# Attention's first blocks stored by two queues and turned sooner, its maxima and queries summed in PSUM, the projections' tiles normalised by ScalarE

## The chip, the cores and the metric

One core of a Trainium2 chip runs the whole program in one launch. Its engines are TensorE (PE), VectorE (DVE), ScalarE (ACT), GpSimd (POOL) and SyncE (SP), which only issues transfers; each works through its own instructions in order and waits on semaphores for the others. The metric is the device time of one execution in microseconds.

## The reference

Four layers, each between a layer norm before and one after, added to the residual. The change touches only the first, attention over 2 sequences of 512 tokens and 32 heads of 16:

```python
x = x + _layernorm(_L0_attn_ref(_layernorm(x), wq, wk, wv, wo))
# _L0_attn_ref, b=2, s=512, H=32, HD=16
q = rotary((x @ wq).reshape(b, s, H, HD)); k = rotary((x @ wk).reshape(b, s, H, HD))
v = (x @ wv).reshape(b, s, H, HD)
scores = jnp.einsum('bqhd,bkhd->bhqk', q, k) * scale
scores = jnp.where(causal[None, None], scores, jnp.finfo(scores.dtype).min)
out = jnp.einsum('bhqk,bkhd->bqhd', jax.nn.softmax(scores, axis=-1), v).reshape(b, s, d)
return out @ wo
```

After it come a feed-forward layer with low-rank terms, a recurrent mixer of four layers, and a feed-forward layer with 4-bit weights.

## The kernel before

Products are made of three fp32r products of a high and a low part (hi·hi, hi·lo, lo·hi), so each operand is split: ScalarE copies it to fp32r, and VectorE or GpSimd subtracts that copy from the source.

**Projections.** Tokens are 8 tiles of 128. For tile t VectorE makes mean and variance (`stats`), GpSimd the inverse deviation (`inv_std`), VectorE the normalised tile `xn` (`norm_x`), TensorE turns it (L1264), ScalarE and VectorE split it into `xt_hi` and `xt_lo`, and TensorE makes q, k and v with 12 products each (L1271), one tile's 36 products two tiles behind the turning. VectorE rotates q and k in two parts (`rope`, L930 and L935) and GpSimd adds them into `qk`, three tiles behind. The weights wq, wk, wv are split in between: the high parts by ScalarE, the low ones by VectorE (L950), one in each of its steps 2, 3 and 4.

**Blocks and stacks.** A block g holds four pairs of heads for all 512 tokens of one sequence, 8 blocks in all, 32 pairs. TensorE turns q and k of a block (`turn_block`, L1277), ScalarE copies the high part (`turned_hi`) and VectorE the low one (`turned_lo`). Twelve transfers store them to `turned` in HBM, each part twice or three times in other rows, and GpSimd's queue loads the result as two tiles of 1 MB with hi and lo stacked over 64 rows (`load_stacks`), so that one product of 64 rows gives a score of all parts. Block 0 is turned within the projections, before the last two tiles (banks 6 and 7); SP stores it, and GpSimd loads it after its last addition to `qk`. It goes to `q_first` and `k_first`, the others to `xt_hi` and `xt_lo`.

**The loop.** `PERIODS` is one list for all engines: each takes from it, in its order, the steps that concern it. A period m works on four pairs: ONE (scores of a tile of queries, with a mask, L1322 and L1326, of which VectorE takes the maxima, L970) for the next two pairs; TWO (transposed scores less the maxima, L1367) for the two pairs now, of which ScalarE takes the exponential (L797) and GpSimd zeroes the corner above the diagonal (L701); PV (probabilities times v, L1378), FLIP (turning the result back, with VectorE's division), TURN (turning half a block, into bank 6) and STACK (loading a block). ONE, TWO and FLIP share a ring of three pairs of banks, and each waits for the reader of the step three before. PLACE brings a pair's maxima under its queries: TensorE multiplies the rows of maxima, `max_row`, with the identity into bank 6 (L1359), and VectorE adds the stack of queries and writes `q_less_max` (L983, out as `w_hi`), which TWO reads. The loop begins with m = −1, where there is only ONE for pairs 0 and 1 and the turning of block 1.

## Time and profile before

| what | us |
|---|---|
| median of 3 runs (868.88, 877.41, 869.16) | 869.16 |
| profiled execution | 873.33 |
| its span in the trace | 871.6 |
| TensorE busy in the span | 763.8 (88%) |
| VectorE | 580.2 (67%) |
| GpSimd | 436.9 (50%) |
| ScalarE | 321.6 (37%) |
| attention, from the start to the last product of its loop | about 310 |
| short steps: VectorE's two on the maxima | 0.21 and 0.17 |
| ScalarE's copy of v, of the identity | 0.60, 0.30 |
| VectorE's remainder of half a block (128x512) | 0.69 |

The span is the time between the first and the last instruction in the trace. Busy times overlap between engines, so shares say who is loaded, and the chain of waits says who is waited for. A row of the timeline gives start, length, engine, line, operation, out<-in with shapes, and in brackets how long the engine had been idle and who ended it. A matmul's recorded length is longer than the step to the next one, since they overlap in the array; so for a series the step between starts counts. "fp32r" products of 512 columns come one after another at 0.23 us.

### The profile page before, as it was taken

To read this page: it belongs to the slowest core of one execution; us is meant where nothing else is said; L and a number is where in the kernel's file an instruction comes from. 1 tells how busy PE (TensorE), PEld (TensorE's weight loads), DVE (VectorE), ACT (ScalarE), POOL (GpSimd) and SP (SyncE) were. 2 spreads that over 40 slices of the span, in tenths; PEclk is the share of its full clock that TensorE was granted. 3 is DMA by queue.
4 is the path that set the end of the run, shared out by engine and by line. 5 is a ranking of instruction groups with operands and counts; after the bars stand their busy time and mean duration, and the time that the engine had idled before them with its cause. 6 is when DMAs were issued, how large, how long until landed. Compare 5 with 4: busy or idle time off the path is not lost.

```text
span 871.6 us, 12853 instructions
## 1 busy us (share of the span) xinstructions
PE 763.8 (88%) x4451; PEld 552.9 (63%) x4451; DVE 580.2 (67%) x1251; ACT 321.6 (37%) x535; POOL 436.9 (50%) x587
## 2 busy tenths in 40 slices
PE   3799688999999887868998898989988999999995
PEld 2578454555555355646886676766766776778883
DVE  5444275888888449996447887889787777580015
ACT  3011044555555544423322432432353342524420
POOL 3233222354333226446645765765686586566632
PEclk9899867999999879979999999999999999999998
DMA  8001463545552040345484332431644131234301
GB/s 304 0 1 34 136 197 121 185 148 155 165 170 97 2 162 1 115 142 184 172 288 161 124 124 91 133 121 63 190 132 121 34 89 48 61 97 145 88 1 48
DMA packets 56944, 101.38 MB, mean 116 GB/s; under 512 B 13616, under 2 KB 17200, under 8 KB 54704
## 3 DMA queue, kind: packets, MB, share of 16 engines
q1 hardware_dynamic: 54576, 83.78, 30.6%
q0 software_dynamic: 2304, 16.78, 5.3%
q8 instruction: 36, 0.59, 0.3%
q14 instruction: 28, 0.23, 0.1%
HBM read 74.58 MB, written 27.00 MB: 117 GB/s over the span
## 4 chain that ended last, share of the span: by engine, by line
PE 54%; DVE 30%; issue 5%; POOL 4%; ACT 4%; DMA 3%; SPq 0%; DVEq 0%; ACTq 0%; POOLq 0%
PE psum L1456 18%; PE psum L1476 11%; PE psum L1271 7%; DVE negmax L970 5%; PE psum L1378 3%; PE psum L1367 3%; DVE bnst L1038 2%; ACT probs L797 2%; DVE w_hi L983 2%; DVE stage_w L1130 2%; PE psum L1507 2%; DVE hn L1210 1%; PE psum L1322 1%; DVE x L1051 1%; DMA xt_lo<-turned 1%
## 5 line engine op out<-in xcount | busy, mean ns | idle before, releaser
L1456 PE MATMUL psum<-xt_hi,wgu_hi 128*128 128x512 f32 (+1 forms) x352 | 142.7, 405 | 0.0
L1456 PE MATMUL psum<-xt_hi,wgu_lo 128*128 128x512 f32 (+1 forms) x352 | 141.8, 403 | 0.0
L1456 PE MATMUL psum<-xt_lo,wgu_hi 128*128 128x512 f32 (+1 forms) x352 | 141.3, 401 | 0.0
L725 POOL TENSOR_TENSOR wgu_lo<-raw,wgu_hi 128x512 fp32r<-128x512 f32 (+1 forms) x88 | 116.9, 1335 | 32.3 <-ACT wgu_hi L857 32.1
L970 DVE TENSOR_REDUCE negmax<-psum 128x2 f32<-128x1024 f32 (+3 forms) x128 | 104.0, 820 | 33.6 <-PE psum L1326 31.6
L701 POOL TENSOR_SCALAR_AFFINE_SELECT probs<-probs 128x256 f32<-128x256 f32 x128 | 52.1, 407 | 140.1 <-ACT probs L797 140.0
L797 ACT ACTIVATE probs<-psum 128x1024 f32<-128x1024 f32 (+3 forms) x128 | 89.0, 704 | 86.2 <-PE psum L1367 84.6
L1109 DVE TENSOR_TENSOR hf<-sg,psum 128x512 f32<-128x512 f32 (+1 forms) x44 | 30.0, 683 | 81.7 <-PE psum L1456 55.2
L725 POOL TENSOR_TENSOR wd_lo<-raw,wd_hi 128x512 fp32r<-128x512 f32 (+1 forms) x44 | 58.2, 1333 | 40.3 <-ACT wd_hi L864 40.1
L730 POOL TENSOR_TENSOR h_lo<-hf,h_hi 128x512 fp32r<-128x512 f32 (+1 forms) x44 | 59.1, 1344 | 37.1 <-ACT h_hi L878 37.1
L1476 PE MATMUL psum<-wd_hi,h_hi 128*128 128x512 f32 (+1 forms) x176 | 73.4, 417 | 4.2 <-POOL h_lo L730 3.7
L1456 PEld LDWEIGHTS psum<-xt_hi,wgu_lo 128*128 128x128 f32 (+1 forms) x352 | 66.4, 189 | 16.6
L1456 PEld LDWEIGHTS psum<-xt_hi,wgu_hi 128*128 128x128 f32 (+1 forms) x352 | 66.3, 188 | 15.4 <-POOL wgu_lo L725 0.2
L1456 PEld LDWEIGHTS psum<-xt_lo,wgu_hi 128*128 128x128 f32 (+1 forms) x352 | 66.3, 188 | 15.1
L857 ACT ACTIVATE wgu_hi<-raw 128x512 fp32r<-128x512 f32 (+1 forms) x88 | 53.2, 616 | 46.4 <-PE psum L1456 24.2
L1476 PE MATMUL psum<-wd_hi,h_lo 128*128 128x512 f32 (+1 forms) x176 | 70.2, 399 | 0.0
L1476 PE MATMUL psum<-wd_lo,h_hi 128*128 128x512 f32 (+1 forms) x176 | 70.0, 398 | 0.0
L1378 PE MATMUL psum<-probs,v 128*32 128x128 f32 (+3 forms) x512 | 51.6, 477 | 4.3 <-POOL probs L701 3.6
L1367 PE MATMUL psum<-w_hi,xt_lo 64*128 64x512 f32 (+2 forms) x224 | 46.3, 412 | 5.4 <-DVE w_hi L983 3.7
L670 POOL TENSOR_TENSOR qk<-rot_c,rot_s 128x512 f32<-128x512 f32 x16 | 21.1, 1316 | 57.1 <-DVE rot_s L935 57.1
L878 ACT ACTIVATE h_hi<-hf 128x512 fp32r<-128x512 f32 (+1 forms) x44 | 27.7, 630 | 57.6 <-DVE hf L1109 56.7
L710 POOL TENSOR_SCALAR ve<-mv 128x1 f32<-128x1 f32 x56 | 16.2, 290 | 63.2 <-DVE mv L1039 36.7
(202 smaller groups left out, 1581.7 us busy)
## 6 DMA issues: line engine op xcount, KB each, us to landing
raw<-full SPq DMA_DIRECT2D x60, 256.0 KB, 2.7
raw<-in_gu_t SPq DMA_DIRECT2D x40, 256.0 KB, 3.8
stage_w<-in_w SPq DMA_DIRECT2D x30, 256.0 KB, 3.2
full<-stage_w SPq DMA_DIRECT2D x30, 256.0 KB, 2.0
turned<-w_hi SPq DMA_DIRECT2D x56, 128.0 KB, 3.4
xt_hi<-turned POOLq DMA_DIRECT2D x7, 1024.0 KB, 5.1
xt_lo<-turned POOLq DMA_DIRECT2D x7, 1024.0 KB, 7.7
turned<-w_lo SPq DMA_DIRECT2D x28, 128.0 KB, 2.4
```

The costliest lines, as they stand in the source:

```text
L701: nc.gpsimd.affine_select(out=diagonal, in_=diagonal, pattern=[[0, 2], [1, P]], compare_op=ALU.is_ge, fill=0.0, base=0, channel_multiplier ...
L725: nc.gpsimd.tensor_tensor(lo, src, hi.bitcast(F32), ALU.subtract).then_inc(sem("w_lo"), 1)
L730: nc.gpsimd.tensor_tensor(h_lo[0:n, r % RING, :], hf[0:n, r % 2, :], h_hi[0:n, r % RING, :].bitcast(F32), ALU.subtract).then_inc(sem("h_lo ...
L797: nc.scalar.activation(probs_of(e)[:, :, 0:(TB - i) * P], pair_of_banks(e)[:, :, 0:(TB - i) * P], ACT.Exp).then_inc(sem("exp"), 1)
L857: nc.scalar.activation(wgu_hi[:, (2 * r + c) % 4, :, 0:n], src.rearrange("p (k h) -> p k h", k=KD)[:, :, 0:n], ACT.Copy).then_inc(sem("w_h ...
L970: nc.vector.tensor_reduce(negmax[:, g, i, :], pair_of_banks(e)[:, :, 0:(i + 1) * P], AX_X, ALU.max, negate=True).then_inc(sem("row_max"), 1)
L1109: nc.vector.tensor_tensor(hf[0:n, r % 2, :], sg[0:n, r % 2, :], bank[(2 * r + 1) % 3][0:n, :], ALU.mult).then_inc(sem("full"), 1)
L1271: ins = nc.tensor.matmul(dst, lhs(i, k), rhs(j, k), start=start and n == 0, stop=stop and n == len(todo) - 1)
L1367: ins = nc.tensor.matmul(pair_of_banks(e)[:, h, 0:(TB - i) * P], k_stack(g)[rows, i * P:(i + 1) * P], q_less_max(g)[rows, i * P:S], start= ...
L1378: ins = nc.tensor.matmul(bank[7][32 * four:32 * four + 32, i * P:S], v[:, TB * b + i, col:col + 32], probs_of((TWO, pair, i))[:, h, 0:(TB ...
L1456: ins = nc.tensor.matmul(bank[q % 3][0:n, :], (wgu_hi, wgu_lo)[hi_w][:, q % 4, k, 0:n], XT[hi_x][:, k, ch * 512:ch * 512 + 512], start=ite ...
L1476: ins = nc.tensor.matmul(bank[3 + j % 2][:, :], (h_hi, h_lo)[lo_h][0:n, r % RING, j * P:(j + 1) * P], (wd_hi, wd_lo)[lo_w][0:n, r % RING, ...
```

## The change

1. ScalarE makes `xn` instead of VectorE, as x·rstd + (−mean·rstd); GpSimd computes the bias in one more step (`ve[:, 7]`). ScalarE's order is: tile t+1 normalised, then tile t copied.
2. The stores of blocks 0 and 1 are split: SP issues the six of q (j = 0), ScalarE's queue the six of k (j = 1). Later blocks stay with SP.
3. GpSimd loads block 0 before its last two additions to `qk`, instead of after them.
4. Both halves of block 1 are turned at once at the loop's start, into banks 6 and 7, and its load is taken up at the start of period 0.
5. PLACE: TensorE first multiplies the stack of queries with the identity into bank 6 and adds the maxima to it there; ScalarE copies the sum. VectorE's addition is gone.

```diff
-            ahead = 1 if m < 0 else m // 2 + 2 if m % 2 == 0 else 0
+            ahead = m // 2 + 2 if m >= 0 and m % 2 == 0 else 0
             stack = m // 2 + 1 if m % 2 == 0 else 0
-            todo = [(STACK, stack * (m > 0), 0), (TWO, now_a, 0), (ONE, next_a, 3), (PLACE, now_b, 0),
+            todo = [(TURN, int(m < 0), 0), (TURN, int(m < 0), 1), (STACK, stack, 0), (TWO, now_a, 0), (ONE, next_a, 3), (PLACE, now_b, 0),
                     (TWO, now_a, 1), (ONE, next_a, 2), (PV, m - 1, 3), (TWO, now_b, 0), (TURN, ahead, 0), (ONE, next_a, 1),
-                    (STACK, stack * (m == 0), 0), (TWO, now_b, 1), (ONE, next_a, 0), (PV, m, 0), (TURN, ahead, 1),
+                    (TWO, now_b, 1), (ONE, next_a, 0), (PV, m, 0), (TURN, ahead, 1),
...
+        def turn_bank(g, i):
+            return bank[6 + i if g == 1 else 6]
...
+        def store_turned(queue, G, j, part):
+            block, ready = ((turned_hi(G), "block_hi"), (turned_lo(G), "block_split"))[part]
+            queue.wait_ge(sem(ready), 2 * G + j if G else 1)
+            for h in range(2):
+                for copy in range(3):
+                    if part == (copy == 2 - j):
+                        row = 64 * h + HD * copy
+                        queue.dma_start(turned[G % 2, j, row:row + HD].rearrange("r p n -> (r p) n"),
+                                        block[64 * h:64 * h + 64, j, :].bitcast(F32)).then_inc(sem(f"turned_out{G % 2}"), 16)
...
+                for part in range(2):
+                    for j in range(2 if G > 1 else 1):
+                        store_turned(sp, G, j, part)
...
-                nc.gpsimd.tensor_tensor(rstd[:, n, t:t + 1], ve[:, n, t:t + 1], neghalf[:, 0:1], ALU.pow).then_inc(sem(done), 1)
...
+                link(nc.gpsimd.tensor_tensor(rstd[:, n, t:t + 1], ve[:, n, t:t + 1], neghalf[:, 0:1], ALU.pow))
+                nc.gpsimd.tensor_scalar(ve[:, 7, t:t + 1], mv[:, n, t, 0:1], rstd[:, n, t:t + 1], -1.0, ALU.mult, ALU.mult).then_inc(sem(done), 1)
...
+                if t == NT + ROPE_LAG - 1:
+                    pool.wait_ge(sem("stack_rows_in"), 8 * 16)
+                    load_stacks(0)
...
-            pool.wait_ge(sem("stack_rows_in"), 8 * 16)
-            load_stacks(0)
...
+            def norm_x(t):
+                act.wait_ge(sem("x_rstd0"), t + 1)
+                if t >= 2:
+                    act.wait_ge(sem("xt_psum0"), t - 1)
+                nc.scalar.activation(xn[:, t % 2, :], x[:, t, :], ACT.Identity, bias=ve[:, 7, t:t + 1], scale=rstd[:, 0, t:t + 1]).then_inc(sem("xn0"), 1)
+
+            norm_x(0)
             for t in range(NT + 2):
+                if t + 1 < NT:
+                    norm_x(t + 1)
                 if t < NT:
                     xt_tile(0, t)
...
                     nc.scalar.activation(turned_hi(0), psum[:, 6:8, :], ACT.Copy).then_inc(sem("block_hi"), 1)
+                    store_turned(act, 0, 1, 0)
+                    store_turned(act, 0, 1, 1)
...
+                    if g == 1 and i == 1:
+                        store_turned(act, 1, 1, 0)
+                        store_turned(act, 1, 1, 1)
...
+                elif what == PLACE:
+                    act.wait_ge(sem("placed"), g + 1)
+                    nc.scalar.activation(q_less_max(g), bank[6][:, :], ACT.Copy).then_inc(sem("q_less_max"), 1)
...
-                elif what == PLACE:
-                    dve.wait_ge(sem("placed"), g + 1)
-                    nc.vector.tensor_tensor(q_less_max(g), bank[6][:, :], q_stack(g).bitcast(F32), ALU.add).then_inc(sem("q_less_max"), 1)
...
+                    nc.tensor.matmul(bank[6][:, :], ident_r[:, :], q_stack(g), start=True, stop=False)
                     for t in range(TB):
-                        ins = nc.tensor.matmul(bank[6][:, t * P:(t + 1) * P], max_row[:, t, :], ident_r[:, :], start=True, stop=True)
+                        ins = nc.tensor.matmul(bank[6][:, t * P:(t + 1) * P], max_row[:, t, :], ident_r[:, :], start=False, stop=t == TB - 1)
```

Where the instructions stand, first on TensorE at the end of the projections, before (L1271 projections, L1322 and L1326 scores of pair 0 with mask, L1277 the turning of block 1's first half):

```order
L1271 MATMUL psum<-w_hi,xt_lo 128x512
L1322 MATMUL psum<-k_first,q_first 128x512 x2
L1326 MATMUL psum<-causal,ident 128x128 x2
L1326 MATMUL psum<-causal,ident 128x64 x2
L1322 MATMUL psum<-k_first,q_first 128x384 x2
L1326 MATMUL psum<-causal,ident 128x128 x2
L1326 MATMUL psum<-causal,ident 128x64 x2
L1277 MATMUL psum<-ident,qk 128x128 x4
```

and now (L1284, L1335 and L1339, L1290 in the same order):

```order
L1284 MATMUL psum<-w_hi,xt_lo 128x512
L1290 MATMUL psum<-ident,qk 128x128 x8
L1335 MATMUL psum<-k_first,q_first 128x512 x2
L1339 MATMUL psum<-causal,ident 128x128 x2
L1339 MATMUL psum<-causal,ident 128x64 x2
L1335 MATMUL psum<-k_first,q_first 128x384 x2
```

The eight transposes of block 1 have moved ahead of all scores. On GpSimd at the same place, before (L670 additions to qk, L682 loads of blocks 0 and 1, L701 corner of the probabilities):

```order
L670 TENSOR_TENSOR qk<-rot_c,rot_s 128x4x4x32 x8
L682 DMA q_first<-turned 128x2048
L682 DMA k_first<-turned 128x2048
L701 AFFINE_SELECT probs<-probs 128x2x128 x3
L682 DMA xt_hi<-turned 128x2048
L682 DMA xt_lo<-turned 128x2048
```

and now (L694, L676, L710):

```order
L694 TENSOR_TENSOR qk<-rot_c,rot_s 128x4x4x32 x6
L676 DMA q_first<-turned 128x2048
L676 DMA k_first<-turned 128x2048
L694 TENSOR_TENSOR qk<-rot_c,rot_s 128x4x4x32 x2
L676 DMA xt_hi<-turned 128x2048
L676 DMA xt_lo<-turned 128x2048
L710 AFFINE_SELECT probs<-probs 128x2x128 x16
```

The load of block 0 has moved ahead of the last two additions, and that of block 1 ahead of the first three corners. On TensorE within a period of the loop, around the placing of a pair's maxima, before (L1359 the placing, L1367 transposed scores):

```order
L1322 MATMUL psum<-xt_lo,xt_hi 128x384 x2
L1326 MATMUL psum<-causal,ident 128x128 x2
L1326 MATMUL psum<-causal,ident 128x64 x2
L1359 MATMUL psum<-ident_r,max_row 128x128 x4
L1367 MATMUL psum<-w_hi,xt_lo 128x128 x2
L1322 MATMUL psum<-xt_lo,xt_hi 128x256 x2
```

and now (L1371 the queries, L1373 the maxima, L1381 transposed scores):

```order
L1335 MATMUL psum<-xt_lo,xt_hi 128x384 x2
L1339 MATMUL psum<-causal,ident 128x128 x2
L1339 MATMUL psum<-causal,ident 128x64 x2
L1371 MATMUL psum<-xt_hi,ident_r 128x512
L1373 MATMUL psum<-ident_r,max_row 128x128 x4
L1381 MATMUL psum<-w_hi,xt_lo 128x128 x2
L1335 MATMUL psum<-xt_lo,xt_hi 128x256 x2
```

One product of 512 columns has been added ahead of each placing; there are 32 of them.

## Rows read from the trace of the kernel before

**Rows 1.** Timeline of the projections: start, length, engine, line, operation, [idle <-releaser]

```profile
15.70 1.12 PE L1264 MATMUL psum<-ident,xn 128*128 128x128 f32 x4 [3.09 <-DVE xn L914]
30.05 0.80 PE L1271 MATMUL psum<-w_hi,xt_hi 128*128 128x512 f32 x1 [5.88 <-DVE w_lo L950]
44.11 0.66 PE L1264 MATMUL psum<-ident,xn 128*128 128x128 f32 x4 [0.31 <-DVE xn L914]
11.24 0.61 POOL L656 TENSOR_TENSOR rstd<-ve,neghalf 128x1 f32<-128x1 f32 x1
11.96 2.27 DVE L950 TENSOR_TENSOR w_lo<-w_raw,w_hi 128x2048 fp32r<-128x2048 f32 x1
26.41 0.79 DVE L914 TENSOR_SCALAR xn<-x,mv,rstd 128x512 f32<-128x512 f32 x1
```

**Rows 2.** Timeline, end of the projections: stores and load of block 0

```profile
82.56 7.52 SPq L570 DMA_DIRECT2D turned<-y  x12
97.64 0.40 PE L1271 MATMUL psum<-w_lo,xt_hi 128*128 128x512 f32 x1
97.87 0.40 PE L1271 MATMUL psum<-w_hi,xt_lo 128*128 128x512 f32 x1
98.17 0.79 POOL L682 DMA_DIRECT2D q_first<-turned  x1
106.09 0.80 PE L1322 MATMUL psum<-k_first,q_first 64*128 64x512 f32 x2 [7.82 <-DMA k_first<-turned]
```

**Rows 3.** Timeline, maxima of pairs 0 and 1, first transposed scores

```profile
107.18 2.09 DVE L970 TENSOR_REDUCE negmax<-psum 128x2 f32<-128x1024 f32 x2 [9.78 <-PE psum L1326]
110.12 1.01 DVE L970 TENSOR_REDUCE negmax<-psum 128x2 f32<-128x512 f32 x2
115.47 0.79 PE L1367 MATMUL psum<-w_hi,k_first 64*128 64x512 f32 x2 [0.33 <-DVE w_hi L983]
```

**Rows 4.** Timeline, load of block 1, starts of periods 1 and 2

```profile
121.35 0.56 POOL L682 DMA_DIRECT2D xt_hi<-turned  x1
128.82 0.50 PE L1367 MATMUL psum<-w_hi,k_first 64*128 64x512 f32 x2 [0.42 <-DVE negmax L970]
132.83 0.79 PE L1322 MATMUL psum<-xt_lo,xt_hi 64*128 64x512 f32 x2 [3.50 <-DMA xt_lo<-turned]
146.91 0.50 PE L1367 MATMUL psum<-w_hi,xt_lo 64*128 64x512 f32 x2
```

**Rows 5.** Busy by stretch: PE, PEld, DVE, ACT, POOL, PEclk, DMA share, GB/s

```profile
118.00:120.00 2.00, 2.00 (x12) 1.23 (x13) 1.66 (x3) 1.01 (x2) 0.41 (x1) 0.50 0.12 28
150.00:200.00 50.00, 46.73 (x491) 26.62 (x490) 40.70 (x75) 29.26 (x46) 19.78 (x43) 1.00 0.58 197
```

**Rows 6.** The same view while block 0 is stored

```profile
84.00:86.00 2.00, 2.00 (x11) 1.59 (x10) 1.35 (x3) 0.00 (x0) 0.27 (x1) 1.00 0.91 209
```

**Rows 7.** Timeline of a period of the loop, and the last period's start

```profile
189.78 0.34 PE L1322 MATMUL psum<-xt_lo,xt_hi 64*128 64x384 f32 x2
190.15 0.66 PE L1359 MATMUL psum<-ident_r,max_row 128*128 128x128 f32 x4
192.47 0.50 PE L1367 MATMUL psum<-w_hi,xt_lo 64*128 64x512 f32 x2
193.46 0.66 PE L1359 MATMUL psum<-ident_r,max_row 128*128 128x128 f32 x4
194.53 0.68 DVE L983 TENSOR_TENSOR w_hi<-psum,xt_hi 128x512 fp32r<-128x512 f32 x1
194.54 0.81 ACT L797 ACTIVATE probs<-psum 128x768 f32<-128x768 f32 x1 [0.50 <-PE psum L1367]
195.25 0.59 ACT L803 ACTIVATE heads_t<-psum 128x512 f32<-128x512 f32 x1
195.89 1.02 ACT L797 ACTIVATE probs<-psum 128x1024 f32<-128x1024 f32 x1
293.49 0.50 PE L1367 MATMUL psum<-w_hi,xt_lo 64*128 64x512 f32 x2
```

## What I predicted before the changed kernel ran

> **What bounds the kernel now.** I read the chain of waits first, for the stretch before 310 us, since every edit lies there; then the timeline at each place where that chain leaves TensorE. Three places show.
>
> In the projections TensorE first starts at 15.70, having waited 3.09 us for a normalised tile from VectorE; it stands still again for 5.88 us before 30.05, until VectorE has split wv; and it waits 0.31 us before 44.11 and before two more tiles [rows 1]. At the end it has its last product at 97.87 and then nothing until 106.09, where the first scores wait for the stacked block 0 [rows 2]. Call the end of the projections E: 97.87 + 0.23 = 98.1 (0.23 is the step from one product to the next [rows 2]). Block 1 is late too: its load is issued at 121.35 and lands just before 132.83, after 3.5 us of standing [rows 4]. The granted clock after such a rest is 0.50, that is 1.2 GHz, as at 118 to 120 [rows 5]; the same pair of score products takes 0.79 us there and 0.50 later [rows 3, 4].
>
> From 146.91, the first transposed scores of period 2, to 293.49, those of period 15, the loop runs evenly: 13 periods in 146.58 us, 11.28 each [rows 4, 7]. There the chain changes between TensorE, VectorE and ScalarE, and no engine alone is the bound.
>
> **Term 1, the projections' start: −3.0.** GpSimd has the rate of tile 2 at 11.85 [rows 1]. It now adds one small step (about 0.3, as its other one-column steps), ScalarE normalises in 0.6, so TensorE can turn tile 2 from about 12.8 to 13.9. VectorE's split of wq began at 11.96 and takes 2.27 [rows 1]; without the tile ahead of it (0.5) it ends at 13.8. The first product starts at 13.9, against 15.70 + 0.7 = 16.4: 2.5 us. After the first tile's rotation VectorE no longer normalises a tile at 26.41 (0.79 long, 0.7 to its successor) before it splits wv: 0.7 more. That is 3.2. ScalarE now has two tiles to normalise around its own copies of the weights, which can delay the split of wk; the bounds are 0.7 (only the second part) and 3.5. I take 3.0.
>
> **Term 2, the tiles: −0.9.** ScalarE normalises tile t+1 before it copies tile t, a whole tile ahead, so the three waits of 0.31 go [rows 1]. What is late next is nothing: TensorE then runs from product to product. So E′ = E − 3.9.
>
> **Term 3, from E to period 2: −16.6.** Now this takes 146.91 − 98.1 = 48.8. With the change:
> - Load of block 0. Its stores were issued from 82.56 for 7.52 us by one queue [rows 2], so landed by about 92. The load was issued at 98.17 only because it stood behind the last two sums of GpSimd, and the scores began 7.9 later. It now stands ahead of these sums: issued at E′ − 8 (two queues halve the 7.5) to E′ − 6 (they don't), it lands at E′ − 0.1 to E′ + 1.9.
> - Block 1 is turned at once, in both banks. ScalarE copies the last v (0.6, as the heads [rows 7]) and the identity (a quarter of the columns, 0.3), and after the hand-overs starts the halves at E′ + 1.1; two copies of 0.6 and VectorE's last remainder (0.7, as its addition [rows 7]) end at E′ + 3.0. Block 0 is there by then under either bound, so the load's price is nothing; were it 3 us later still, each us would count.
> - Eight row maxima. Four reductions take 2.09 + 1.01 = 3.1 [rows 3], 2.95 with their overlaps, and the two small steps on the maxima, with hand-over, just under 0.5. Pair 0 is done at E′ + 6.4, the third-last reduction of pair 1 at E′ + 8.4, and the ring of banks lets the first transposed scores start at E′ + 8.5 (now 115.47, E + 17.4 [rows 3]). The two remainders that lay between reductions are ahead of them.
> - Period 0 took 128.82 − 115.47 = 13.35 at mostly half clock [rows 3, 4]. At full clock I take 12.4, an even period with a turning (about 11.9) plus the first wait for a maximum. The load of block 1 falls into this period: its stores are all issued by E′ + 6.1 from two queues, E′ + 9.3 if they don't help, landed 2 later; the load then takes 7.8 as block 0's [rows 2] to 11.4 as block 1's beside the next stores (121.35 to 132.7 [rows 4]). It lands between E′ + 16 and E′ + 22.8, and is wanted at E′ + 21.2. I take no stall; the bound is 1.6.
> - Period 1 took 146.91 − 132.83 = 14.1 from its first new score, half of it at low clock; now 11.3.
> The sum is 8.5 + 12.4 + 11.3 = 32.2, so 48.8 − 32.2 = 16.6. What could spoil it is the clock: between E′ + 1.3 and E′ + 8.5 TensorE has only some 4 us of work. If it falls to 0.50 there and comes back in period 1, period 0 costs its old 13.35 (+0.9), the maxima some 1 more and period 1 about 1.4 more: 3.3.
>
> ScalarE issues six of the stores of block 1 from E′ + 2.3 to E′ + 6.1 (0.63 each, 7.52 / 12). Behind them stands its copy of pair 0's query, which TensorE gives at E′ + 7.4: it waits for no one.
>
> The Trainium skill speaks against the second queue: in DMA: Bandwidth & Descriptors, Issuing engines are not separate DMA queues, all queues run on the same 16 DMA engines, and issuing from several saves only the sequencer's time. The row at 84 to 86 us agrees in part, since those engines are already 0.91 busy at 209 GB/s with one queue [rows 6]. By the rule the stores of both blocks end at the later of the bounds above, which costs up to the 1.6 us stall and nothing else.
>
> **Term 4, the loop: +5.1.** Each pair's maxima now need one product more on TensorE, 128x512, 0.23 by the step in [rows 2]. VectorE loses its 0.68 addition (0.60 to the next) and ScalarE gets a copy of 0.6, as its copy of the heads (0.59) [rows 7]. I follow a period, in which this happens twice.
> - Pair a of the next period. TensorE goes from the scores at 189.78 over the placing at 190.15 to the transposed scores at 192.47 with hardly a pause, 2.69 [rows 7]: placing, two scores, P·V, transposed scores, scores. VectorE's reductions end just before each is wanted, so its 0.60 was a second chain of equal length. Taking it away gains nothing; the product adds 0.23, 0.21 after a small pause.
> - Pair b. Before, from 192.47: the reduction, the addition at 194.53, then the exponential of pair b at 195.89, 3.42 after. Now ScalarE does, in its order: the exponential of pair a (0.92 from 0.55 on), a wait for the placing, the copy, an exponential of 768 (0.71), the heads (0.50), the exponential of pair b. The placing at 193.46, 0.99 after, ends 0.66 + 0.23 later, so the copy runs from 1.91 to 2.43, and pair b starts at 2.43 + 0.72 + 0.50 = 3.65 against 3.42: 0.23.
> So +0.43 in a period. Where a block is turned as well TensorE stands for VectorE's remainder between its two halves, and part is absorbed: 0.3. With 8 periods of the first kind, 5 of the second and 0.2 in the last: 3.4 + 1.5 + 0.2 = 5.1. Bounds: 0, if the slack in both places is larger than I read, and 9.5, if a product costs its whole recorded 0.40 [rows 2].
>
> **Sum.** −3.9 − 16.6 + 5.1 = −15.4. The profiled execution took 873.33 (span 871.6), so 857.9 by it; the median of the runs shown is 869.16, 4.2 lower, which gives 853.8. I forecast 855, since part of the 3.3 for the clock is likely.
>
> **Rivals.**
> - *Forecast, 0.55*: early gain of 17 to 20.5, the loop gives back 3 to 7. 851 to 859.
> - *The loop gives nothing back, 0.15*: VectorE is busy for most of every period, and its two additions appear on the chain of waits in each. Against it stands the walk above. Unchanged loop: 869.2 − 20.5 = 848.7; if both additions came off the chain, 14 × 1.2 = 17 less, 832. The Trainium skill has this rule in Perfetto Trace Analysis, Optimizing Scalar/DVE Operations: with VectorE saturated, moving work to ScalarE may make sense. The trace bears it out only if ScalarE's order leaves room, and its row at 194.54 leaves none.
> - *The early gain is smaller, 0.22*: clock at 0.50 (3.3) and the load of block 1 as slow as now (1.6), after which period 1 restarts as it did (2.8 more at most): 855 + 7 = 862, up to 866 with the upper bound of term 4.
> - *Slower, 0.04*: the loop loses the full clock because TensorE's pauses grow. Periods at low clock cost 14.1 against 11.3 at least 2.8 more each; with 15.4 in hand it decides from the sixth such period, and all 13 give 855 + 36 = 891. Against it: 1.00 was granted from 150 to 200 [rows 5], and TensorE only gets more to do.
> - *The change doesn't do what it says, 0.04*: the first scores still wait for a load, 869 − 3.9 + 5.1 = 870.
>
> **How the numbers follow.** About 1% is what a measurement of this kernel can tell from no change. Faster by more (under 860.5): 0.55 + 0.15 + 0.05 of the third = 0.75. Within 1%: 0.17 + 0.04 = 0.21. Slower: 0.04. The range leaves out the best of the second case and the worst of the third: 848 to 864.
>
> **What would show it.** First product at about 14; wv's split ending near 27; no waits before the tiles; E′ near 94.2; first scores within 2 us of E′ and no wait for stacked rows after; period 2 at E′ + 32. Periods of 11.2 to 11.3 without a turning and about 12.2 with one; ScalarE without idle time before the heads' copy. Wrong if periods get shorter, or if the clock row shows 0.50 after E′, or if TensorE waits for block 1.

## The result: 1.2% faster, and the profile after

The changed kernel took 859.07 us (median of 857.41, 858.31, 859.83 and 865.05), the kernel before 869.43 beside it: a ratio of 0.988, with an interval of 0.984 to 0.993. A second set of six runs, on another occasion, gave 859.06 and 0.986 (0.981 to 0.991). The forecast was 855 (848 to 864).

| us | before | after | difference |
|---|---|---|---|
| first product of the projections | 16.47 | 15.11 | −1.36 |
| first product with wv | 30.05 | 28.45 | −1.60 |
| E, end of the projections | 98.10 | 95.53 | −2.57 |
| from E to period 2 | 48.81 | 35.59 | −13.22 |
| 13 periods of the loop, 2 to 15 | 146.58 | 151.13 | +4.55 |
| from period 15 to the end of the span | 578.1 | 575.85 | −2.25 |
| span of the profiled execution | 871.6 | 858.1 | −13.5 |

E, the way to period 2 and the loop add up to −2.57 − 13.22 + 4.55 = −11.24; the two first products are parts of E. The −2.25 behind period 15 is not the change's: but for one last placing the code there is the same, and in the profiled executions of this study that part lasts from 571.8 to 579.7 us. The medians differ by 10.4, where the forecast had a gain of 14.2 (869.2 to 855). Of the −1.36, 0.5 is not the change's either: VectorE could begin the statistics of tile 2 at 9.41, when its input had landed, and at 9.94 before. From there to the first product it takes 5.70 us, and took 6.53.

The start of the projections, as a timeline of the kernel after (start, length, engine, line, operation, idle time and its releaser):

```profile
11.02 2.29 DVE L966 TENSOR_TENSOR w_lo<-w_raw,w_hi 128x2048 fp32r<-128x2048 f32 x1
11.38 2.06 POOL L664 TENSOR_SCALAR ve<-mv,rstd 128x1 f32<-128x1 f32 x1
13.47 0.81 ACT L775 ACTIVATE xn<-x,ve,rstd 128x512 f32<-128x512 f32 x1 [2.49 <-POOL ve L664]
14.34 1.12 PE L1277 MATMUL psum<-ident,xn 128*128 128x128 f32 x4 [4.47 <-ACT xn L775]
15.11 0.78 PE L1284 MATMUL psum<-w_hi,xt_hi 128*128 128x512 f32 x1
15.19 0.26 POOL L664 TENSOR_SCALAR ve<-mv,rstd 128x1 f32<-128x1 f32 x1
...
26.10 2.38 POOL L662 TENSOR_SCALAR ve<-mv 128x1 f32<-128x1 f32 x1
26.11 2.28 DVE L966 TENSOR_TENSOR w_lo<-y,w_hi 128x2048 fp32r<-128x2048 f32 x1
28.45 0.80 PE L1284 MATMUL psum<-w_hi,xt_hi 128*128 128x512 f32 x1 [5.19 <-DVE w_lo L966]
33.74 0.66 PE L1277 MATMUL psum<-ident,xn 128*128 128x128 f32 x4
```

These answer to [rows 1]. The new step on GpSimd (L664), one column, takes 2.06 us for tile 2, and 0.26 for the next tile. TensorE's idle time ahead of the normalised tile 2 now ends at 14.34 (before at 15.70), and that ahead of wv at 28.45 (30.05). Before the later tiles (33.74, and two more) no wait is left, where there were 0.31 us each.

The end of the projections and the first scores, the same view; queue rows (SPq, ACTq) give how long the issuing took:

```profile
80.05 5.24 SPq L550 DMA_DIRECT2D turned<-y  x6
80.06 5.75 ACTq L550 DMA_DIRECT2D turned<-y  x6
88.75 0.79 POOL L676 DMA_DIRECT2D q_first<-turned  x1 [1.45 <-issue]
95.30 0.39 PE L1284 MATMUL psum<-w_hi,xt_lo 128*128 128x512 f32 x1
96.22 0.30 ACT L799 ACTIVATE ident_r<-ident 128x128 fp32r<-128x128 f32 x1
96.73 1.06 PE L1290 MATMUL psum<-ident,qk 128*128 128x128 f32 x8 [1.04 <-issue]
97.72 0.50 PE L1335 MATMUL psum<-k_first,q_first 64*128 64x512 f32 x2
102.61 0.17 DVE L995 TENSOR_TENSOR max_row<-negmax,max_row 128x8 fp32r<-128x8 f32 x1
105.40 0.77 PE L1381 MATMUL psum<-w_hi,k_first 64*128 64x512 f32 x2
106.18 0.58 POOL L676 DMA_DIRECT2D xt_hi<-turned  x1 [10.50 <-DMA turned<-w_lo]
120.34 0.49 PE L1335 MATMUL psum<-xt_lo,xt_hi 64*128 64x512 f32 x2
```

These answer to [rows 2 to 4]. The load of block 0 is issued 6.8 us before E (88.75), and the first scores start 2.2 us after E (97.72) instead of 8.0. About a second of those 2.2 us is a wait of TensorE before the turning of block 1, ending at 96.73 just after ScalarE's copy of the identity, for which TensorE's program waits ahead of the whole loop. The load of block 1 is issued at 106.18, and the scores that need it start at 120.34 with no wait.

The granted clock in this stretch and, in the last row, in the loop, in the kernel after (length of the stretch, busy time of PE, PEld, DVE, ACT and POOL, then PEclk, DMA share, GB/s):

```profile
98.00:100.00 2.00, 0.99 (x18) 0.66 (x16) 1.85 (x3) 0.54 (x2) 0.00 (x0) 1.00 0.41 97
100.00:102.00 2.00, 0.94 (x12) 0.58 (x12) 2.00 (x4) 0.00 (x0) 0.00 (x0) 1.00 0.94 222
102.00:104.00 2.00, 2.00 (x14) 1.47 (x11) 1.93 (x6) 0.00 (x0) 0.00 (x0) 0.53 0.97 274
114.00:116.00 2.00, 2.00 (x12) 1.15 (x8) 0.00 (x0) 0.45 (x1) 0.00 (x0) 0.56 0.66 160
...
150.00:200.00 50.00, 47.40 (x489) 27.12 (x485) 36.34 (x64) 30.69 (x50) 22.75 (x45) 1.00 0.47 149
```

From 98 to 102 TensorE was busy for half of the time (its scores wait until VectorE has taken the maxima from the banks), and from 102.1 to 115.8 it was granted 0.50, that is 1.2 GHz, though it is busy throughout (0.53 in the stretch from 102 and 0.56 in that from 114 are mixtures of the two levels). Afterwards it has 1.00 again, in the loop too. There VectorE is busy for 36.34 us of 50, against 40.70 before [rows 5].

The start of period 2, of the two periods behind it and of period 15, and ScalarE's exponential of pair b in period 2:

```profile
131.12 0.47 PE L1381 MATMUL psum<-w_hi,xt_lo 64*128 64x512 f32 x2
134.86 1.05 ACT L820 ACTIVATE probs<-psum 128x1024 f32<-128x1024 f32 x1
143.40 0.47 PE L1381 MATMUL psum<-w_hi,xt_lo 64*128 64x512 f32 x2
154.61 0.48 PE L1381 MATMUL psum<-w_hi,xt_lo 64*128 64x512 f32 x2
282.25 0.48 PE L1381 MATMUL psum<-w_hi,xt_lo 64*128 64x512 f32 x2
```

A period with a turning lasts 143.40 − 131.12 = 12.28 us and one without 11.21; before, the same two lasted 11.92 and 10.87 (from 146.91 to 158.83 and to 169.70). The exponential of pair b (134.86) starts 3.74 us after the period does, where before it started 3.42 after [rows 7].

### The profile page after: what moved, and what is told of

It is laid out like the page before. It is cut to its first block, busy times and chain, and to the rows that moved or that the text cites. A ratio compares the mean times of both kernels' runs of the same rounds, so it can differ in the third digit from the quotient of the medians.

```text
span 858.1 us, 12930 instructions
## 1 busy us (share of the span) xinstructions
PE 763.4 (89%) x4483; PEld 553.1 (64%) x4483; DVE 558.2 (65%) x1211; ACT 341.1 (40%) x575; POOL 441.7 (51%) x595
## 4 chain that ended last, share of the span: by engine, by line
PE 60%; DVE 24%; issue 6%; ACT 5%; POOL 4%; DMA 1%; SPq 0%; DVEq 0%; ACTq 0%
PE psum L1470 19%; PE psum L1490 11%; PE psum L1284 9%; PE psum L1392 5%; ACT probs L820 3%; PE psum L1381 2%; DVE bnst L1051 2%; PE psum L1371 2%; PE psum L1335 2%; DVE negmax L986 2%; DVE stage_w L1143 2%; PE psum L1373 2%; PE psum L1521 2%; DVE hn L1223 1%; DVE x L1064 1%
## 5 line engine op out<-in xcount | busy, mean ns | idle before, releaser
L710 POOL TENSOR_SCALAR_AFFINE_SELECT probs<-probs 128x256 f32<-128x256 f32 x128 | 52.1, 407 | 122.8 <-ACT probs L820 122.7
L1335 PE MATMUL psum<-xt_lo,xt_hi 64*128 64x512 f32 (+1 forms) x224 | 40.9, 362 | 7.4 <-ACT probs L820 5.8
L897 ACT ACTIVATE sg<-psum 128x512 f32<-128x512 f32 (+1 forms) x44 | 26.2, 595 | 53.6 <-PE psum L1467 27.0
```

Source lines behind the costliest of these rows:

```text
L710: nc.gpsimd.affine_select(out=diagonal, in_=diagonal, pattern=[[0, 2], [1, P]], compare_op=ALU.is_ge, fill=0.0, base=0, channel_multiplier ...
L1335: nc.tensor.matmul(dst[:, h, :], lhs[rows, :], rhs[rows, :], start=True, stop=False)
```

## The experiments

All start from the changed kernel unless said otherwise, and all times of stages come from one profiled execution each. Here they are in one table; p2 − E is the time from the end of the projections to period 2, the loop is the 13 periods, and the ratio is that to the kernel before, run beside it. Each stage comes from a single execution, each median from 4 to 10.

| run | E | first score | p2 − E | loop | median us | ratio (interval) |
|---|---|---|---|---|---|---|
| kernel before | 98.10 | 106.09 | 48.81 | 146.58 | 869.43 | |
| changed kernel | 95.53 | 97.72 | 35.59 | 151.13 | 859.07 | 0.988 (0.984–0.993) |
| placing as before | 94.98 | 97.17 | 35.18 | 146.63 | 854.19 | 0.983 (0.977–0.988) |
| copy on VectorE | 96.55 | 98.75 | 35.57 | 149.60 | 856.27 | 0.985 (0.978–0.991) |
| unread products | 97.41 | 99.64 | 32.37 | 151.10 | 858.49 | 0.987 (0.982–0.992) |
| VectorE waits for GpSimd | 94.49 | 96.69 | 35.44 | 151.12 | 863.18 | 0.995 (0.991–0.998) |
| one queue of stores | 93.57 | 95.82 | 35.31 | 151.07 | 860.01 | 0.988 (0.981–0.995) |
| load of block 0 late | 94.81 | 104.71 | 42.53 | 151.06 | 867.49 | 0.996 (0.992–0.999) |
| block 1 late | 94.12 | 95.34 | 39.87 | 151.07 | 861.91 | 0.989 (0.982–0.996) |
| VectorE normalises | 98.09 | 100.29 | 34.41 | 151.08 | 862.75 | 0.991 (0.988–0.994) |
| placing as before + products | 94.56 | 96.76 | 32.38 | 146.50 | 851.02 | 0.977 (0.973–0.982) |
| the same, identity earlier | 95.93 | 97.20 | 31.13 | 146.54 | 851.29 | 0.978 (0.973–0.983) |
| changed kernel again | 94.80 | 97.00 | 35.38 | 151.09 | 859.06 | 0.986 (0.981–0.991) |

E moves from execution to execution (93.57 to 97.41 among those in which ScalarE normalises), and the part behind the loop by several us. The landing of the inputs is one reason for the scatter of E, but not the only one: with one queue of stores the first product comes 0.2 us later than in the changed kernel (15.29 and 15.11), but the step from product to product falls from 0.43 to 0.23 us already at 17.5 instead of 20, and wv's first product comes 1.1 earlier (27.37 and 28.45). The loop, which depends on neither, repeats within 0.15 us, and p2 − E within 0.4 in the six executions in which the clock falls and both loads stand as in the changed kernel (with one exception, told below). So stages are judged by the trace first and the medians are a second, coarser witness.

### The placing as before (fifth part undone)

```diff
-   nc.scalar.activation(q_less_max(g), bank[6][:, :], ACT.Copy).then_inc(sem("q_less_max"), 1)
+   nc.vector.tensor_tensor(q_less_max(g), bank[6][:, :], q_stack(g).bitcast(F32), ALU.add).then_inc(sem("q_less_max"), 1)
...
-   nc.tensor.matmul(bank[6][:, :], ident_r[:, :], q_stack(g), start=True, stop=False)
```

> The changed kernel with its fifth part alone undone: no product of the queries on TensorE, VectorE adds the queries to the maxima as before. Theory A (a period is a chain of TensorE and ScalarE in their orders, and the fifth part lengthens it): periods fall back from 11.22 and 12.28 us to 10.87 and 11.96, the 13 periods from 151.1 to about 146.6, and the whole is 4.5 to 5 us faster than the changed kernel, some 854. Theory B (VectorE's additions were a burden, and the loop's loss in the changed kernel comes from something else, such as its shifted loads): the periods stay above 11.2 or grow, and the whole is not faster.

The 13 periods take 146.63 us, as before (146.58), against 151.13. The median is 4.9 us below that of the changed kernel (854.19 and 859.07). Two periods of it:

```profile
130.16 0.50 PE L1380 MATMUL psum<-w_hi,xt_lo 64*128 64x512 f32 x2
133.01 0.49 PE L1380 MATMUL psum<-w_hi,xt_lo 64*128 64x512 f32 x2 [0.29 <-DVE w_hi L996]
142.08 0.50 PE L1380 MATMUL psum<-w_hi,xt_lo 64*128 64x512 f32 x2
152.94 0.50 PE L1380 MATMUL psum<-w_hi,xt_lo 64*128 64x512 f32 x2
```

11.92 and 10.86. Here pair b's transposed scores (133.01) do wait 0.29 us for VectorE's addition, and yet the period is shorter than the one without the addition. So the fifth part costs all that the loop gives back, and the other four cost the loop nothing.

### Copy on VectorE (the product on TensorE alone)

The sum in PSUM stays, but VectorE copies it, not ScalarE:

```diff
-   nc.scalar.activation(q_less_max(g), bank[6][:, :], ACT.Copy).then_inc(sem("q_less_max"), 1)
+   nc.vector.tensor_copy(q_less_max(g), bank[6][:, :]).then_inc(sem("q_less_max"), 1)
```

> The changed kernel, but VectorE instead of ScalarE copies the sum out of bank 6; TensorE still multiplies the queries by the identity. It splits the loss of 0.35 a period into the product's part and ScalarE's part. If TensorE's product costs at one of the two places only (0.2) and ScalarE's order costs the rest, periods are 10.9 to 11.1 without a turning and about 12.1 with one. If the product costs all, they stay at 11.2 and 12.3. If ScalarE's order costs all, they are back at 10.87 and 11.96.

```profile
132.12 0.49 PE L1381 MATMUL psum<-w_hi,xt_lo 64*128 64x512 f32 x2
134.29 0.68 DVE L996 CAST w_hi<-psum 128x512 fp32r<-128x512 f32 x1
144.28 0.49 PE L1381 MATMUL psum<-w_hi,xt_lo 64*128 64x512 f32 x2
155.38 0.49 PE L1381 MATMUL psum<-w_hi,xt_lo 64*128 64x512 f32 x2
```

Periods of 12.16 and 11.10, 149.60 in all. The copy takes VectorE 0.68 us, as long as the addition did, so this version differs from the old placing by the product on TensorE alone: 149.60 − 146.63 = 2.97, or 0.23 a period. That is one step of TensorE, although a period has two such products. Moving the copy to ScalarE adds 1.53 more, 0.12 a period. Both halves of the fifth part lose. ScalarE's exponential of pair b shows both too: it starts 3.38 us after the period does with the old placing, 3.60 in this version and 3.74 in the changed kernel.

### Unread products while TensorE waits for maxima

Thirteen products into a bank that nobody reads are put among the scores of pairs 0 and 1. No other result depends on them. Ahead of each group TensorE waits until block 1 is split, a wait that can only delay it.

```diff
+   FILL = {(0, 0): 6, (1, 3): 2, (1, 1): 2, (1, 0): 3}
...
+   if FILL.get((g, i)):
+       pe.wait_ge(sem("block_split"), 3)
+       for _ in range(FILL[g, i]):
+           nc.tensor.matmul(bank[7][:, :], ident_r[:, :], q_stack(0), start=True, stop=True)
```

> The changed kernel with 13 products more that nothing reads (128x512, queries of block 0 by the identity, into bank 7): 6, 2, 2 and 3 of them before the scores of tiles (0,0), (1,3), (1,1) and (1,0), where TensorE now waits for VectorE. If the half clock from 102 to 115 us in the changed kernel comes from TensorE's rests there, the granted clock stays at 1.00 or comes back sooner, and period 2 begins 2 to 3.5 us earlier after the projections than now (35.4). If the rests do not decide it, the clock falls as it does now and the products cost up to 1 us.

```profile
98.00:100.00 2.00, 1.36 (x12) 1.07 (x14) 0.00 (x0) 1.04 (x4) 0.00 (x0) 1.00 0.00 0
100.00:102.00 2.00, 1.48 (x21) 1.11 (x20) 1.94 (x3) 0.45 (x1) 0.00 (x0) 1.00 0.45 107
102.00:104.00 2.00, 2.00 (x13) 1.13 (x11) 2.00 (x4) 0.00 (x0) 0.00 (x0) 1.00 0.94 229
```

The granted clock stays 1.00 where the changed kernel has 0.50, and p2 − E falls from 35.59 to 32.37, though TensorE has more to do. The low clock therefore costs about 3 us: 3.2 in this pair, 3.0 against the changed kernel's second profile, 2.8 between the two versions with the old placing (35.18 and 32.38). E is 1.9 us later here, so the stretches above do not stand at the same distance from it as those of the changed kernel. Counted in both from 2.5 us after E, TensorE is busy for 1.48 and 2.00 us of two stretches of 2 us, against 0.99 and 0.94. The median (858.49, against 859.07) does not show the gain: the single runs of both scatter by more. The nearest comparison is further below, 854.19 against 851.02; it agrees, but the intervals of the two ratios overlap.

### VectorE waits for GpSimd's step

```diff
    dve.wait_ge(sem("w_split_hi"), t - 1)
+   if t == 2:
+       dve.wait_ge(sem("x_rstd0"), 3)
```

> The changed kernel, but VectorE waits for GpSimd's three steps on tile 2 before it splits wq. In the changed kernel the third of these took 2.06 us instead of 0.27, beside VectorE's 2.29 of splitting. If the two hold each other up (a step of GpSimd stands until VectorE's long subtraction ends), it takes 0.27 here, the split starts 0.6 later, and TensorE turns tile 2 at about 12.8 to 13.2 instead of 14.34, so that the first product comes up to 1 us earlier and wv's split perhaps 0.5. If the 2.06 is only a defect of the record, the tile is turned no earlier and the first products come 0.6 later.

The timeline of this version: the first row is of tile 2, the last two of tile 3, for which there is no such wait:

```profile
12.88 0.26 POOL L664 TENSOR_SCALAR ve<-mv,rstd 128x1 f32<-128x1 f32 x1
...
17.01 2.28 DVE L968 TENSOR_TENSOR w_lo<-y,w_hi 128x2048 fp32r<-128x2048 f32 x1
17.42 2.00 POOL L664 TENSOR_SCALAR ve<-mv,rstd 128x1 f32<-128x1 f32 x1
```

GpSimd's step takes 0.26 us when VectorE holds its subtraction back, and 2.00 when it falls beside the next one. That is the cause of the 2.06 above; in the nine other executions of versions in which ScalarE normalises, without the wait, the step on tile 2 takes 2.00 to 2.29.

Tile 2 landed 1.5 us later in this execution than in the changed kernel's first profile (statistics from 10.91 and 9.41), so the first product, at 15.69, must be compared with an execution of like landing. The changed kernel's second profile is one: statistics from 10.81, first product at 16.45. Against it the wait brings the first product 0.9 us forward, counted from the statistics, wv's 0.5 (28.04 and 28.54) and E 0.3 (94.49 and 94.80). The median, 863.18, is 4 above the changed kernel's all the same. In the profiled execution the stages up to period 15 are not longer, and all the excess lies behind them, where the part lasts 579.7 us against 575.9 and 571.8. Why the medians differ so is open.

### One queue of stores (second part undone)

```diff
-   store_turned(act, 0, 1, 0)
-   store_turned(act, 0, 1, 1)
...
-   for j in range(2 if G > 1 else 1):
+   for j in range(2):
```

ScalarE's six stores of block 1 go in the same way.

> The changed kernel with its second part alone undone: SP issues all twelve stores of blocks 0 and 1. If the second queue only saves issue time that nothing waits for (theory A), block 0's load still lands before the first scores, block 1's load is issued about 3 us later (109 instead of 106.2) and lands at up to 120 beside the next stores, while it is wanted at 120.3: no stall or one below 1.5 us, and the whole is within 1.5 us of the changed kernel. If the two queues are what brings the blocks in time (theory B), TensorE stands 2 us or more before the first score or before block 1, and the whole is 3 us or more slower.

```profile
107.12 0.58 POOL L676 DMA_DIRECT2D xt_hi<-turned  x1 [13.40 <-DMA turned<-w_lo]
118.10 0.50 PE L1330 MATMUL psum<-xt_lo,xt_hi 64*128 64x512 f32 x2
```

With one queue the load of block 1 is issued 13.6 us after E instead of 10.7, but the scores that need it come only 24.5 after E, with no stall. p2 − E is 35.31 against 35.59. The second queue is worth nothing here.

### The load of block 0 late (third part undone)

```diff
-   if t == NT + ROPE_LAG - 1:
-       pool.wait_ge(sem("stack_rows_in"), 8 * 16)
-       load_stacks(0)
...
+   pool.wait_ge(sem("stack_rows_in"), 8 * 16)
+   load_stacks(0)
```

> The changed kernel with its third part alone undone: GpSimd loads block 0 after its last additions to qk. The load is issued at about 95.7 instead of 88.75 and lands 7.8 later, at 103.5. Theory A (every us of that is on the path): the first scores start 5.8 us later than now (97.7) and, the rest in between at low clock, period 2 begins 4 to 6 us later. Theory B (VectorE's remainders of block 1 and the stores of block 1 hide most): period 2 less than 3 us later.

```profile
94.89 0.79 POOL L676 DMA_DIRECT2D q_first<-turned  x1
104.71 0.79 PE L1334 MATMUL psum<-k_first,q_first 64*128 64x512 f32 x2 [7.62 <-DMA k_first<-turned]
```

The load is issued at E, TensorE waits 7.62 us for it, and p2 − E is 42.53: 7 us more than with the load ahead of two additions. The median agrees (867.49 against 859.07, 8.4). Not all of the 7 is standing still: after the wait the clock is at 0.50 until 121.6, about 20 us in all, where the changed kernel has 13.6.

### Block 1 late (fourth part undone)

```diff
-   ahead = m // 2 + 2 if m >= 0 and m % 2 == 0 else 0
+   ahead = 1 if m < 0 else m // 2 + 2 if m % 2 == 0 else 0
```

and TURN and STACK of block 1 stand in the period where they stood before.

> The changed kernel with its fourth part alone undone: block 1 is turned between the scores of pair 0 as before, and its load stands in the middle of period 0. Theory A (the load is what period 1 waits for): its stores begin about 2.5 us later and the load is issued behind the corners of period 0, near 112 to 113; it lands 8 to 11 us later, near 122, so that TensorE stands 2 to 4 us at the start of period 1 and period 2 begins 3 to 6 us later. Theory B (the earlier first scores alone bring block 1 in time): no stall, period 2 within 1.5 us.

```profile
110.12 0.58 POOL L676 DMA_DIRECT2D xt_hi<-turned  x1
119.82 0.50 PE L1335 MATMUL psum<-xt_lo,xt_hi 64*128 64x512 f32 x2 [1.20 <-ACT probs L820]
118.00:120.00 2.00, 0.80 (x12) 0.52 (x10) 0.81 (x3) 1.41 (x2) 0.77 (x3) 1.00 1.01 364
120.00:122.00 2.00, 2.00 (x13) 1.59 (x14) 1.22 (x1) 0.21 (x1) 0.15 (x1) 0.63 0.92 343
```

The first scores are 1.2 after E instead of 2.2, since no turning stands ahead of them, but the load of block 1 is issued at 110.12, 16.0 after E, and p2 − E is 39.87: 4.3 us more. The median is 2.8 above (861.91). TensorE stands for only 1.2 of the 4.3 us, until 119.82. The row names ScalarE, but the second half of the load, issued at 110.70, took 9.0 us to land, which is about 119.7. The rest is the clock: it falls a second time, at 120.5, and is back at 130.8, and period 1 takes 15.9 us instead of 11.2.

### VectorE normalises (first part undone)

`norm_x` goes back from ScalarE to VectorE, with (x − mean)·rstd, and GpSimd's third step is left out.

> The changed kernel with its first part alone undone: VectorE normalises the projections' tiles. Theory A: the waits of 0.31 us before three tiles are back (0.9), the first product comes at 16.4 and wv's at 30.0 as in the kernel before, so the projections end 2.5 us later, near 98.1, if the loads of x land as there. Theory B: the end of the projections is set by the landing of the weights and of x, which differs between executions, and the edit is worth the 0.9 alone.

```profile
15.36 1.11 PE L1277 MATMUL psum<-ident,xn 128*128 128x128 f32 x4 [3.09 <-DVE xn L930]
29.90 0.79 PE L1284 MATMUL psum<-w_hi,xt_hi 128*128 128x512 f32 x1 [5.88 <-DVE w_lo L966]
44.07 0.66 PE L1277 MATMUL psum<-ident,xn 128*128 128x128 f32 x4 [0.31 <-DVE xn L930]
```

All waits of [rows 1] are back at their old lengths, and E is 98.09, as in the kernel before (98.10). The eleven executions in which ScalarE normalises have E at 95.2 on average and none above 97.41, so the part is worth some 2.9, from only two executions on the one side; the median is 3.7 above the changed kernel's.

p2 − E is 34.41 here, 1 us below the others with a low clock, and the clock is the reason:

```profile
106.00:108.00 2.00, 2.00 (x18) 1.46 (x17) 2.00 (x4) 0.60 (x1) 0.00 (x0) 0.50 0.80 284
116.00:118.00 2.00, 2.00 (x24) 0.99 (x20) 0.29 (x1) 0.92 (x2) 0.00 (x0) 0.94 0.70 209
```

It falls at 106.0, 7.9 us after E (the stretch before still has 1.00), and is back at 116.2: 10.2 us at 0.50, against 13.6 in the changed kernel, where it falls 6.6 after E. TensorE's work ahead of the fall is the same, 0.98 and 0.93 us busy in the two stretches of 2 us from 2.5 us after E. What sets the moment of the fall is not shown.

### The best version, and the identity's copy

The old placing together with the unread products:

> The changed kernel with its fifth part undone and with the 13 unread products: both gains should add, since one lies in the loop and the other before it. Period 2 at 32 to 32.5 after the projections (35.6 in the changed kernel), the 13 periods in 146.6 (151.1), so 7.5 us faster than the changed kernel, some 851 to 852. If the clock's gain depends on the queries' products being there, period 2 stays at 35.

851.02, 0.977 (0.973 to 0.982) of the kernel before: 3.2 below the version without the products, which ran in another set, and 8 below the changed kernel, which ran beside it. The parts add up: p2 − E is 32.38 as with the products alone and the loop 146.50 as with the old placing.

In the second version ScalarE also copies the identity earlier, before it waits for block 0 in the projections:

```diff
    if t == NT:
+       nc.scalar.activation(ident_r[:, :], ident[:, :], ACT.Copy).then_inc(sem("ident_r"), 1)
        act.wait_ge(sem("block_psum"), 1)
...
-   nc.scalar.activation(ident_r[:, :], ident[:, :], ACT.Copy).then_inc(sem("ident_r"), 1)
    act.wait_ge(sem("qk_ready"), 2 * NT)
```

> As the run before, and ScalarE copies the identity ahead of block 0's halves instead of behind the last copy of v. TensorE now stands 1.04 us after its last projection for that copy. If it is what TensorE waits for there, the turning of block 1 starts about 0.9 earlier and period 2 comes 0.5 to 0.9 earlier after the projections, 31.5 to 32; if the last v or the sum of qk decides, nothing changes.

```profile
95.94 1.04 PE L1290 MATMUL psum<-ident,qk 128*128 128x128 f32 x8
97.20 0.50 PE L1335 MATMUL psum<-k_first,q_first 64*128 64x512 f32 x2 [0.23 <-DMA k_first<-turned]
```

TensorE's 1.04 us before the turning are gone, and p2 − E is 31.13, 1.25 less. The median, 851.29, does not show it; a gain of 1 us is below what six runs tell apart.

### The changed kernel again

> The changed kernel itself, unaltered, on the chip and beside the runs of the two above: between 857 and 861, with the 13 periods in 151.1.

859.06, against 859.07 in the first set, with 0.986 for 0.988, and the same stages (35.38 and 151.09). Single runs of a set lie up to 8 us apart (853.93 to 862.21), but the two medians agree far better than the differences of 4.9 and 8 above.

## Why the prediction was right, and which terms were off

The time, 859.07, lies inside the range, 4 us above the 855, between the forecast case (851 to 859) and the rival with a smaller early gain (862). The loop gave back 4.55, as the forecast case had it; the early gain was 15.8, below the 17 to 20.5 of that case. Of the prediction's own signs, "Wrong if … the clock row shows 0.50 after E′" came true: in the clock it was wrong. The other two did not: no period got shorter, and TensorE did not wait for block 1. Step by step:

**What bounds the kernel** held: what moved lies in the first 310 us, at the places where TensorE waited, and nothing behind them moved beyond the scatter between executions.

**Term 1 (−3.0) was mis-sized: −1.6.** Each piece of its chain was right but one. It took GpSimd's new one-column step at about 0.3 us, "as its other one-column steps". On tile 2 it took 2.06. The step (11.38 to 13.44) falls beside VectorE's subtraction on wq (11.02 to 13.31), which no longer has a tile ahead of it. ScalarE's 0.81 instead of 0.6 for the normalised tile took another 0.2. So the first product came at 15.11 and not at 13.9. The same happened at 26.10 (2.38 us for GpSimd's first step, beside the split of wv at 26.11), but no wait of TensorE rests on that one. The split of wv ended at 28.4, not 27, because VectorE came to it late: the first products were late, and its steps on their results with them. The term named the delay of the split by ScalarE as its risk; the delay came from GpSimd. At the first product (−1.36 for −2.5) 0.5 is luck, tile 2's earlier landing.

**Term 2 (−0.9) was right**: the three waits before the tiles, 0.93 together, are gone. Between wv's first product and E it is 0.97 in this pair; over all executions that stretch is 66.2 to 67.1 us, and 68.1 and 68.2 where VectorE normalises, so it may be worth somewhat more. Both together: −2.57 in the profiled pair, −2.9 on average over executions, for −3.9.

**Term 3 (−16.6) was right in mechanism, and short of its size by the clock that it named.** Measured −13.22, 3.4 less. "If it falls to 0.50 there" it put 3.3 on it; it fell, and with the unread products that keep it at 1.00 the stage takes 32.37 where 32.2 was forecast. The sum on which that number rests is not right in its pieces. To the first transposed scores it is 9.9 with the low clock and 10.4 with the products, not 8.5; period 0 at full clock is 10.8, not 12.4; period 1 is 11.2 for 11.3. That the first two errors cancel is luck. A piece of the first is the 1.04 us for which TensorE waits for the identity's copy before it turns block 1; the term let ScalarE copy and TensorE turn beside each other. Pair 0's maxima are done at 102.78, 7.2 after E and not 6.4. The 3.3 for the low clock is right in sum alone, too: it had 0.9 in period 0, 1 in the maxima and 1.4 in period 1. The changed kernel loses all of it in period 0, 14.5 us against 10.8 with the products, nothing to the first transposed scores, and nothing in period 1 (11.2 in both). The forecast ought to have taken the fall of the clock as likely, since it had counted only some 4 us of work in 7 for TensorE; it left the 3.3 out of the sum, and took back a part in the final figure. The clock has a part in the gain itself: before, it was 0.50 for 34 of the 48.8 us (102.5 to 123.0 and, from the wait for block 1 on, 129.8 to 143.5), and now for 13.6 of the 35.6.

Of its parts, the load ahead of the additions is worth 7.0 us, block 1's early turning 4.3, and the second queue nothing; there was no stall on block 1 with either one queue or two. Each part was undone by itself, so these need not add up to the 13.2, and don't. Two queues issued six stores each in 5.24 and 5.75 us, against 7.52 for twelve by one [rows 2], so even the issuing gained only 1.8 of the 3.8 us that halving would give. The Trainium skill says that queues share the DMA engines and that a second one saves sequencer time alone (DMA: Bandwidth & Descriptors, Issuing engines are not separate DMA queues); by that rule, which the prediction weighed, the trace agrees. The stall of 0 to 1.6 was put at 0, and is 0. It is so with the low clock, though: at full clock, with one queue, the load would be wanted some 3 us earlier; this was not tried.

**Term 4 (+5.1) was right**: +4.55 for these 13 periods, +0.36 in a period with a turning and +0.34 in one without, for 0.3 and 0.43. That taking the addition off VectorE gains nothing is what the first two experiments show; that the two chains were of equal length is the prediction's reading of [rows 7]. The division between causes was off: the product costs 0.23 per period and ScalarE's order 0.12 rather than 0.23. ScalarE starts pair b's exponential at 3.74 (3.65 forecast), but 0.22 of the 0.36 us by which that is later than with the old placing come with the product alone, where the term had put all of it on ScalarE's order.

**The rivals.** The loop giving something back (849 or 832) is excluded. VectorE's busy time in 50 us of the loop fell from 40.70 to 36.34 and the periods grew. The Trainium skill's advice to move work to ScalarE when VectorE is saturated (Perfetto Trace Analysis, Optimizing Scalar/DVE Operations) spoke for that rival; the trace does not bear it out here. The rival of a smaller early gain had the right mechanism, the clock, and it held what became of the forecast: the sum of 853.8, + 3.4 in term 3, + 1.3 in terms 1 and 2, − 0.4 in the loop is 858.1, 1 us under the median. The slower ones (clock lost in the loop, first scores still waiting) did not occur.

## What to carry to other kernels

Work taken off a busy engine gains nothing if the receiver stands in order on a chain of equal length, and the product that replaces it is charged for as well (here one of the two in a period); compare the two chains to the next hand-over before moving it. What paid here was not faster work but transfers issued ahead of work that nobody awaited: 7 us for moving a load past two additions, 4.3 for starting the next block earlier. When a gap is closed only half, look at what the clock will do in the stretch that stays half idle, and count that loss in.

## What was not expected of the hardware

- **A one-column step on GpSimd lasts until VectorE's long subtraction beside it ends.** It takes 0.26 us alone (12.88 in the version with the wait). Beside a subtraction of 2.28 us, 128x2048 from two operands in SBUF, it took 2.06 and 2.00, and GpSimd's first step, otherwise 0.22, took 2.38; each ended within 0.15 us of the subtraction. The step at 15.19 took 0.26 too, although VectorE was at a subtraction (128x512, one operand in PSUM, 14.87 to 15.56), so not every one of VectorE's operations holds GpSimd up. Which ones do was not separated.
- **The clock in a thin stretch.** After TensorE had been busy for 0.99 and 0.94 us of two stretches of 2 us the clock fell to 0.50 and came back 13.6 us later, in spite of full work in between. With the unread products, at 1.48 and 2.00 us in the same stretches after E, it stayed at 1.00. Thirteen products that nobody reads were worth about 3 us. With the same work ahead, though, the clock fell 6.6 us after E in the changed kernel and 7.9 after it with VectorE normalising, for 13.6 and 10.2 us.
- **A short wait costs more than itself.** With block 1 late TensorE stood for 1.2 us, and period 1 became 4.6 us longer, because 10 us at 0.50 followed.
- **ScalarE's normalising pass** (128x512, from SBUF, scale and bias per row) took 0.81 us against 0.60 for a copy of the same size from PSUM.
